# Attention values multiplied straight into token order, and the small items put at fewer places between the convolution's steps

## The reference

```
x = x + L0_conv(ln(x))      # spectral mixing
t = t + L0_ffn(ln(t))       # 8 experts, top 2
x = x + L1_conv(ln(x))      # the block that this change is in
t = t + L1_ffn(ln(t))       # 8 experts, top 2, and one shared expert
```

```
y    = relu(conv3x3(x, entry_w) * entry_s + entry_b)      # 256 -> 128 channels
qv   = conv1x1(y, vqk_w, ...);  qh = conv1x1(y, hqk_w, ...)   # 16 channels each
A_v  = softmax over rows    of qv . qv, for each column
A_h  = softmax over columns of qh . qh, for each row
feat = conv1x1(y, val_w, val_s, val_b)                    # the values, 128 channels
s_v  = A_v @ feat;   x_v = s_v * gate_v(mean of s_v)
s_h  = A_h @ x_v;    x_h = s_h * gate_h(mean of s_h)
out  = concat(conv1x1(x_h, end_w, ...), conv1x1(mean(x), il_w, ...))
```

## Time and profile before

| | us |
|---|---|
| runs (three) | 1201.56, 1196.70, 1191.82 |
| median | 1196.7 |
| profiled execution | 1199.71 |
| its span, first to last instruction | 1197.3 |
| passes with convolution | 602 to 819 |
| pass 8 | 819 to 849 |
| passes 9 to 12 | 849 to 897 |

### The profile page before, as it was taken

How to read it: one execution, slowest core, us unless ns; L and a number is a source line. 1 busy time by engine, 2 the same in 40 slices (tenths; PEclk the granted TensorE clock), 3 DMA queues, 4 the chain that set the end, 5 groups by cost and what they waited for, 6 DMA issues and landing times. The chain is left out here.

```text
span 1197.3 us, 19835 instructions
## 1 busy us (share of the span) xinstructions
PE 1025.8 (86%) x5686; PEld 858.5 (72%) x5686; DVE 615.7 (51%) x1712; ACT 528.2 (44%) x1328; POOL 264.1 (22%) x274
## 2 busy tenths in 40 slices
PE   6956669999999999973489999998776799997897
PEld 6956658888888888862256665665535799986787
DVE  5488653323232322226356676555778355554566
ACT  6027264444444444432144344433335466666563
POOL 0000012111111111107522200000000554424655
PEclk9999999999999999995689999997665799998889
DMA  9533501111111111118222301002230344434444
GB/s 354 234 110 136 176 24 49 53 54 54 54 54 53 54 54 54 49 41 268 73 80 79 89 1 53 36 18 71 89 123 1 101 139 140 136 114 150 151 131 132
DMA packets 63237, 114.61 MB, mean 96 GB/s; under 512 B 9827, under 2 KB 43253, under 8 KB 62262
## 3 DMA queue, kind: packets, MB, share of 16 engines
q1 hardware_dynamic: 49910, 77.65, 18.5%
q0 software_dynamic: 12960, 35.41, 10.4%
q10 hardware_dynamic: 288, 0.47, 0.1%
HBM read 73.90 MB, written 39.59 MB: 95 GB/s over the span
## 5 line engine op out<-in xcount | busy, mean ns | idle before, releaser
L574 POOL DMA_INDIRECT experts_rows_sb<-h_rows,ids_i x142 | 134.6, 948 | 751.0 <-POOLq L402 423.1
L761 DVE TENSOR_TENSOR experts_a_sb<-experts_a_sb,experts_bankU 128x512 f32<-128x512 f32 x71 | 48.9, 689 | 224.1 <-PE experts_bankU L180 224.1
L714 ACT ACTIVATE experts_a_sb<-experts_bankG 128x512 f32<-128x512 f32 (+1 forms) x142 | 70.0, 493 | 93.0 <-PE experts_bankG L180 91.2
L705 ACT ACTIVATE experts_hT<-experts_bankH 128x256 fp32r<-128x256 f32 x142 | 54.5, 384 | 89.6 <-PE experts_bankH L634 89.5
L727 ACT ACTIVATE experts_y_sb<-experts_bankY 128x256 f32<-128x256 f32 x142 | 54.8, 386 | 87.7 <-PE experts_bankY L177 65.3
L178 PE MATMUL attn_bankC<-attn_padded,attn_w_high 128*128 128x512 f32 x144 | 76.4, 530 | 19.8 <-ACT attn_feat L1432 14.6
L1136 POOL DMA_INDIRECT attn_y<-y_rows,pos_i x64 | 63.9, 998 | 112.2 <-DVE x_res L1562 57.2
L834 POOL DMA_INDIRECT shared_y<-y_rows,pos_i x64 | 65.4, 1022 | 63.9 <-DVE x_res L943 32.1
L177 PE MATMUL experts_bankY<-down_plain,experts_aT_plain 128*128 x284 | 72.9, 379 | 0.0
L183 DVE TENSOR_TENSOR experts_aT<-experts_bankA,experts_aT 128x256 fp32r<-128x256 f32 x142 | 59.6, 420 | 24.1 <-ACT experts_aT L722 24.1
L641 PE MATMUL experts_bankA<-konst_sb,experts_a_sb 128*128 128x128 f32 x426 | 70.0, 273 | 0.4 <-DVE experts_aT L183 0.4
(11 more groups left out here) (365 smaller groups left out, 2853.5 us busy)
## 6 DMA issues: line engine op xcount, KB each, us to landing
y_rows<-experts_y_sb SPq DMA_DIRECT2D x142, 128.0 KB, 1.7
h_rows<-xn SPq DMA_DIRECT2D x32, 256.0 KB, 2.4
x_res<-in_x SPq DMA_DIRECT2D x4, 1024.0 KB, 12.3
mix_xT<-in_xt SPq DMA_DIRECT2D x4, 1024.0 KB, 14.1
gate_raw<-in_L_ffn_gate_w SPq DMA_DIRECT2D x1, 4096.0 KB, 14.2
up_raw<-in_L_ffn_up_w SPq DMA_DIRECT2D x1, 4096.0 KB, 23.5
x_rows<-x_res SPq DMA_DIRECT2D x16, 256.0 KB
x_res<-x_rows SPq DMA_DIRECT2D x8, 512.0 KB, 4.6
```

What stands on the lines that cost most here:

```text
L574: nc.gpsimd.indirect_dma_start(rows[t % DEPTH][:, :], None, h_dram, bass.IndirectOffsetOnAxis(ap=ids_i[:, t:t + 1], axis=0)).then_inc(s_ro ...
L714: nc.scalar.activation(a_sb[i % RING][:, :], bankG[i % RING][:, 0:hidden], ACT.Silu if gate is not None else ACT.Relu).then_inc(s["act"], 1)
L761: nc.vector.tensor_tensor(a_sb[i % RING][:, :], a_sb[i % RING][:, :], bankU[i % RING][:, 0:hidden], ALU.mult).then_inc(s["a"], 1)
```

## The change

The values are made with tokens on the partitions at once. `feat` is written in column order (the ReLU copy is two activations of 256 columns). `project_values` loads blocks of `feat` and streams `val_w`: a bias matmul first, then four products, in the form of `finish`. The value scale is multiplied into `val_w` in `tables`, the bias goes into a third section of `bias_rows`. The transposes of the values, their buffer `val_t` and their semaphore are gone; `values` is the ReLU itself. As `feat` is in column order, the `down` queries are copied by one activation of 512, the `along` queries by two of 256 that go back to row order: three activations where there were five. Two small loads (`val_sb`, `out_rows`) are dropped, `scales_b` is half as wide again.

The small items stand at 8 places between steps of the convolution instead of 15, after every second step.

```diff
                 def project_values(p):
...
-                    nc.tensor.matmul(bankF[:, :], val_w[:, :], feat[:, :], start=True, stop=True).then_inc(s["projected"], 1)
+                    nc.tensor.matmul(bankF[:, :], ones2[:, :], bias_rows[:, 2 * F:3 * F].unsqueeze(1).broadcast_to([2, 4, F]), start=True, stop=False)
+                    for t in range(4):
+                        last = nc.tensor.matmul(bankF[:, t * P:(t + 1) * P], feat[:, t * P:(t + 1) * P], val_w[:, :], start=False, stop=(t == 3))
+                    last.then_inc(s["projected"], 1)
...
-                def turn_values(p):
-                    if not has(p):
-                        return
-                    for t in range(4):
-                        last = nc.tensor.transpose(bankV[:, t * P:(t + 1) * P], val_t[:, t * P:(t + 1) * P], K("ident"))
-                    last.then_inc(s["values_t"], 1)
...
                     finish(i - 4)
                     convolve(i, 0, 2)
                     gate_layer(i - 2, 0)
-                    convolve(i, 2, 3)
                     project_queries(i - 1)
-                    convolve(i, 3, 4)
                     project_values(i - 1)
-                    convolve(i, 4, 5)
+                    convolve(i, 2, 4)
                     turn_rows(i - 5, 0)
                     gate_layer(i - 2, 1)
-                    convolve(i, 5, 7)
+                    convolve(i, 4, 6)
                     turn_rows(i - 5, 1)
                     gate_layer(i - 2, 2)
-                    convolve(i, 7, 8)
                     scores(i - 1, "down")
-                    convolve(i, 8, 9)
+                    convolve(i, 6, 8)
                     turn(i + 1, 0)
                     route(i - 5, 0, 0)
                     gate_layer(i - 2, 3)
-                    convolve(i, 9, 10)
                     scores(i - 1, "along")
-                    convolve(i, 10, 11)
+                    convolve(i, 8, 10)
                     route(i - 5, 0, 1)
+                    route(i - 5, 1, 0)
                     gate_layer(i - 2, 4)
-                    route(i - 5, 1, 0)
-                    convolve(i, 11, 12)
-                    turn_values(i - 1)
+                    convolve(i, 10, 12)
                     route(i - 5, 1, 1)
-                    convolve(i, 12, 13)
                     branch(i)
                     gate_layer(i - 2, 5)
-                    convolve(i, 13, 14)
+                    convolve(i, 12, 14)
                     turn(i + 1, 1)
                     turn_probs(i - 1, "down")
                     turn_logits(i - 5)
-                    convolve(i, 14, 15)
                     turn_probs(i - 1, "along")
-                    convolve(i, 15, 16)
+                    convolve(i, 14, 16)
                     turn_gated(i - 2)
-                    convolve(i, 16, 17)
                     attend_down(i - 1)
-                    convolve(i, 17, 18)
+                    convolve(i, 16, 18)
                     attend_along(i - 2)
...
-                    nc.scalar.activation(feat[:, :], bankC[:, :], ACT.Relu, bias=entry_sb[:, 1:2], scale=entry_sb[:, 0:1]).then_inc(s["feat"], 1)
+                    for n in range(2):
+                        part = slice(n * 256, (n + 1) * 256)
+                        last = nc.scalar.activation(feat[:, part].rearrange("p (h y z) -> p h y z", h=2, y=ROWS), by_column(bankC[:, part]), ACT.Relu,
+                                                    bias=entry_sb[:, 1:2], scale=entry_sb[:, 0:1])
+                    last.then_inc(s["feat"], 1)
...
+                    nc.scalar.activation(q["down"][:, :], bankQ[0:G, :], ACT.Relu, bias=qk_sb[0:G, 1:2], scale=qk_sb[0:G, 0:1])
                     for n in range(2):
                         part = slice(n * 256, (n + 1) * 256)
...
-                    nc.scalar.activation(q["along"][:, :], bankQ[32:32 + G, :], ACT.Relu, bias=qk_sb[32:32 + G, 1:2],
-                                         scale=qk_sb[32:32 + G, 0:1]).then_inc(s["queries"], 1)
+                        last = nc.scalar.activation(by_column(q["along"][:, part]), bankQ[32:32 + G, part].rearrange("p (h y z) -> p h y z", h=2, y=ROWS),
+                                                    ACT.Relu, bias=qk_sb[32:32 + G, 1:2], scale=qk_sb[32:32 + G, 0:1])
+                    last.then_inc(s["queries"], 1)
...
-                    nc.scalar.activation(val[:, :], bankV[:, :], ACT.Copy).then_inc(s["values"], 1)
+                    nc.scalar.activation(val[:, :], bankF[:, :], ACT.Relu).then_inc(s["values"], 1)
...
                     nc.vector.tensor_tensor(end_w[:, :], end_w[:, :], scales_b[:, 0:F], ALU.mult)
+                    nc.vector.tensor_tensor(val_w[:, :], val_w[:, :], scales_b[:, 2 * F:3 * F], ALU.mult)
```

More of the change, by code:

```diff
@@ L977, in attention @@
             s = {n: sem(f"attn_{n}") for n in ("border", "w_high", "w_low", "mask", "tables", "sum", "chain", "var", "log", "root", "rstd", "xn", "turned", "high", "lows", "conv",
-                                               "feat", "projected", "queries", "values_t", "values", "probs_sb", "along_sb", "att",
+                                               "feat", "projected", "queries", "values", "probs_sb", "along_sb", "att",
                                                "att_sb", "row_sums", "gated", "gated_t", "gated_sb", "att2", "feat2", "col_sums",
@@ L1033, in attention @@
             table = {"down": "same_col", "along": "same_row"}
-            bias_raw = sb("attn_bias_raw", [2, 2 * F], on=on)
-            bias_part = [sb(f"attn_bias_part{n}", [2, 2 * F], HALF, on=on) for n in range(2)]
-            bias_rows = sb("attn_bias_rows", [2, 2 * F], HALF, on=on)
+            bias_raw = sb("attn_bias_raw", [2, 3 * F], on=on)
+            bias_part = [sb(f"attn_bias_part{n}", [2, 3 * F], HALF, on=on) for n in range(2)]
+            bias_rows = sb("attn_bias_rows", [2, 3 * F], HALF, on=on)
             ones2 = sb("attn_ones2", [2, P], HALF, on=on)
@@ L1042, in attention @@
             bankP = {"down": bankQ, "along": bankF}
-            bankV, bankO, bankE = bankF, bankS["down"], bankS["along"]
+            bankO, bankE = bankS["down"], bankS["along"]
             GATES = PAIRS + 1
@@ L1096, in _ @@
                 load_x(1)
-                sp.dma_start(bias_raw[:, :], A["out_rows"][:, 2 * F:4 * F].broadcast_to([2, 2 * F])).then_inc(loads["attn"], 16)
+                sp.dma_start(bias_raw[:, :], A["out_rows"][:, 3 * F:6 * F].broadcast_to([2, 3 * F])).then_inc(loads["attn"], 16)
                 load_attention(sp)
@@ L1453, in queries @@
                     act.wait_ge(s["projected"], p + 1)
-                    if p:
-                        act.wait_ge(s["values_t"], p)
+                    nc.scalar.activation(q["down"][:, :], bankQ[0:G, :], ACT.Relu, bias=qk_sb[0:G, 1:2], scale=qk_sb[0:G, 0:1])
                     for n in range(2):
                         part = slice(n * 256, (n + 1) * 256)
-                        nc.scalar.activation(q["down"][:, part].rearrange("p (h y z) -> p h y z", h=2, y=ROWS),
-                                             by_column(bankQ[0:G, part]), ACT.Relu, bias=qk_sb[0:G, 1:2], scale=qk_sb[0:G, 0:1])
-                        nc.scalar.activation(val_t[:, part].rearrange("p (h y z) -> p h y z", h=2, y=ROWS),
-                                             by_column(bankF[:, part]), ACT.Relu, bias=val_sb[:, 1:2], scale=val_sb[:, 0:1])
-                    nc.scalar.activation(q["along"][:, :], bankQ[32:32 + G, :], ACT.Relu, bias=qk_sb[32:32 + G, 1:2],
-                                         scale=qk_sb[32:32 + G, 0:1]).then_inc(s["queries"], 1)
+                        last = nc.scalar.activation(by_column(q["along"][:, part]), bankQ[32:32 + G, part].rearrange("p (h y z) -> p h y z", h=2, y=ROWS),
+                                                    ACT.Relu, bias=qk_sb[32:32 + G, 1:2], scale=qk_sb[32:32 + G, 0:1])
+                    last.then_inc(s["queries"], 1)
                 def values(p):
@@ L2273, in layouts @@
         "il_w": t(a["L1_conv_il_w"].reshape(KC, P, F).transpose(1, 0, 2).reshape(P, -1)),
-        "out_rows": t(np.concatenate([a[f"L1_conv_{n}"] for n in ("end_s", "il_s", "end_b", "il_b")])[None]),
+        "out_rows": t(np.concatenate([a[f"L1_conv_{n}"] for n in ("end_s", "il_s", "val_s", "end_b", "il_b", "val_b")])[None]),
         "L1_ffn_w_router": by_contracted_row(a["L1_ffn_w_router"][None]),
```

17 lines of the change are left out of this document (6 added, 11 removed).

## The result

| | before | after |
|---|---|---|
| median of 20 runs, us | 1194.14 (1187.80 to 1201.56) | 1184.43 (1176.71 to 1193.11) |
| ratio, 95% interval | 1 | 0.991 (0.9888 to 0.9932) |
| span of the profiled execution, us | 1197.3 | 1181.4 |

The two spans differ by 15.9 us, so a part of that difference is not in the medians. I split the spans in three. Up to the first convolution of pass 1: 601.93 before, 597.45 after (-4.5). From there to the first routing matmul: 301.26 and 292.97 (-8.3). The rest: 294.11 and 290.98 (-3.1). The middle part holds the edited passes. Of the edit only small things lie ahead of it: the feature copy of pair 0, the scaling of `val_w` and two loads fewer.

A forecast was written before the change was run, and what follows sets the result against it. TensorE was taken to bound the passes with convolution, chains of three engines pass 8. Terms -4.0 + 1.4 - 1.0 - 1.65 + 0.7 + 0.2 = -4.35 us off the median 1196.7 gave 1192.4, range 1185 to 1201.

The forecast's parts named there:

- breaks: Fewer breaks between convolution steps save TensorE 0.67 us in passes 2 to 4, 0.96 in 5 to 7, 0.10 in 1.
- stall: TensorE waits 0.35 us for VectorE's `leaky` of layer 4, ahead of gate layer 5, in passes 2 and 4: +0.7 us.
- not kept: Gains at the end of passes 4 and 5 are lost waiting for VectorE's sums at gate layer 0: +0.2 us.
- row waits: Waits for copied rows, about 0.32 us each in passes 5 to 7, go with ScalarE's shorter query chain: -1.0 us.
- feature copy: Splitting ScalarE's copy in two delays the next pass's convolution by 0.24 us in each of six passes: +1.4 us.
- The signs: Passes 5 and 6 0.6 to 1.0 us shorter; wrong if seven passes move over 6 us or change lies outside 602-897.
- Rival 1: Grouped items on TensorE still pay their breaks: it loses 1.0 us instead of gaining 4.0, 1197.4 us; chance 0.22.
- The direct values on TensorE: Bias matmul and four products cost 1.43 us against 1.29 for old matmul and transposes: 0.14 more per pair.
- Pass 8: Shorter ScalarE chain less later values gives -0.6 us, transposes gone at half clock give -1.05: together -1.65 us.
- Rival 3: TensorE keeps full clock in pass 8 after a wait of 2.2 us, giving back 5 to 6 us: 1186.5; chance 0.14.
- Rival 2: ScalarE's feature copy and VectorE's gate chain bound each pass: +2.2 to +3.8 us, 1199 to 1200.5; chance 0.14.
- Rival 4: ScalarE's idle times in the last stage that no engine releases move, 5 us either way: 1187 or 1198; chance 0.12.

The follow-up runs named there:

- places alone: The kernel before with the 8 places of the new order, values still transposed: 1153.14 us, ratio to before 0.9892, and 0.9888 when timed again.
- values alone: The kernel after with the 15 places of before, so only the direct values are new: 1166.16 us, ratio to before 1.0011.
- e4: The kernel before with only `attend_down` moved ahead of step 17 of the convolution, 14 places: 1190.96 us, before 1191.04 on that chip.
- e8: Places alone with `attend_down` moved behind the convolution's last step in passes 1 to 3: 1152.73 us, ratio to before 0.9885.
- e5: The kernel before with the ReLU feature copy in two activations of 256 columns, row order kept: 1195.46 us, before 1191.04 on that chip.

## Why the prediction was right or wrong

What failed, in short. The sum has two halves. The terms of the places (breaks -5.0, stall +0.7, not kept +0.2) make -4.1 us; on the second kind of chip places alone measured -13.0 and -13.3 (the medians above). The terms of the direct values (+1.0, +1.4, -1.0, -1.65) make -0.25; alone they measured -0.3 (1.0011, interval 0.9993 to 1.0030), but on top of the places +6.6. So the places were priced too low, and the values added on top too favourably; on those chips the two misses partly cancel (-6.5 for the whole, -4.35 forecast), which is luck.

Three steps inside the passes are named below: the move of `attend_down` was put at nothing without a reason (0.75 us), a wait was priced by the idle time shown (0.32 for 0.49), and costs were charged where they arise though a later wait takes them in (0.5). In the profiles of places alone 8.4 and 7.4 us of the gain lie in passes 1 to 7 and 3.6 and 5.5 in passes 8 to 12 (against the second execution of before); there the granted clock differs (in pass 8 0.71 and 0.84, against 0.61), and how much of that is the change's is open. The 7.4 are accounted for nearly in full: the 4.1 forecast, 1.5 of row waits (which the sum had with the values, at 1.0), 0.75 by `attend_down` and the stall of 0.7 that places alone hasn't got make 7.05. And 2.6 us of the distance from the forecast 1192.4 aren't the change's: it was taken off a median of three runs, 1196.7, and that of twenty is 1194.1.

By its own sum, pass by pass (the forecast of each is its terms added up; the feature copy's sixth 0.24 lies ahead of pass 1):

| pass | forecast | after - before, first executions | second executions |
|---|---|---|---|
| 1 | +0.28 | -0.39 | -0.09 |
| 2 | +0.06 | -0.19 | -0.41 |
| 3 | -0.29 | -0.37 | -0.34 |
| 4 | +0.06 | -0.02 | -0.01 |
| 5 | -0.81 | -1.57 | -1.56 |
| 6 | -1.05 | -1.69 | -1.73 |
| 7 | -1.15 | -2.29 | -2.28 |
| 8 | -1.65 | -2.81 | -3.89 |

**The signs.** The prediction named passes 1 to 7 moving by more than 6 us together as a sign of being wrong: they moved by 6.5. So did a change outside the edited stretch: 7.6 us of the first two spans lie there. Passes 5 and 6 got shorter by 1.6 and 1.7 us, not by 0.6 to 1.0, and pass 1 got shorter, not longer. The transposes are gone from pass 8, and its wait on the rows is 1.93 (2.2 forecast).

**The breaks: right in the price of each.** Priced as in the prediction, pass 7's items between convolution steps came to 15.57 us before and to 14.10 with places alone. Of the 1.47 gained, 0.51 is the row wait (second rows and layer 2 took 1.37, first rows and layer 1, which don't wait, 0.86; below). The rest, 0.96, is what was forecast, in part by luck, as the terms show. Junction by junction: gate layer 0, queries and values 2.27 where they were 0.54 + 1.19 + 0.86 (-0.32, forecast 0.29); layer 2 and scores 2.19 for 0.86 + 1.50 (-0.17; 0.19); layer 3 and scores 2.28 for 0.94 + 1.50 (-0.16; 0.19); transposes, route, branch and layer 5 2.40 for 1.16 + 1.43 (-0.19; 0.19); route next to route 1.38 for 1.48 (-0.10, which I had not counted); the turned probabilities -0.05 (0.10); two full-array items next to each other +0.03 (0). Rival 1, that the breaks don't pay, fell. By the rule on changes of tiling mode (the Trainium skill, "TensorEngine Tiling (Array Packing)", section "Key Properties") a group of unlike items would have kept its drains, and the sum by it was 0.27 us for a late pass. The trace doesn't agree with that sum: 0.96.

**The direct values on TensorE: right alone, too dear in the group.** With their own break they cost 1.49 against 0.86 + 0.44 for matmul and transposes, +0.19 (forecast +0.14, bound 0.23). In the group of after, 2.74 - 2.27 = 0.47 is paid for 0.45 saved (2.40 - 1.95 where the transposes stood): +0.02.

**The row waits: right that they end, the price too low, the second cause missed.** I put their end down to ScalarE's shorter chain. Values alone bears that out, but places alone ends them too, which I had not seen: the two edits share one gain. And I took the idle time shown, 0.32 us, for the price. TensorE of before, pass 5:

```profile
730.12 0.43 PE L180 MATMUL attn_bankC<-attn_padded,attn_w_low 128*128 128x512 f32 x1
730.87 0.63 PE L1297 MATMUL attn_bankT<-konst_sb,xn 128*128 128x128 f32 x4 [0.32 <-ACT moe_xT L1441]
```

From start to start it is 0.75, where a full-array item enters at 0.26: the wait costs 0.49. The profile counts idle time from the modelled end of the matmul before; in a stream the next would have started before that end. Three waits give 1.5 and not 1.0 us.

**The feature copy: right in size, wrong in where it is paid.** By itself it puts +0.23 ahead of five passes, as forecast; in passes 5 and 6 it is taken out of a wait that follows, 0.24 each, so about 0.5 us too much was charged. The wait that is late next was in the earlier trace rows, and I used it only against the gains. In after the wait ahead of pass 2 even fell, from 3.29 to 2.73, as it did with places alone (2.72): ScalarE starts that copy 26.35 us after pass 1's first matmul where it was 26.97. No term had this.

**What was left out: `attend_down`, -0.75 in pass 7.** The diff moves it one step forward, and the sum has no term for the move: TensorE does the same work. VectorE's chain behind it ends the pass. In the profile it was to be seen as idle time of VectorE behind L1226, followed by 4.54 us without a gap.

**Pass 8: the terms right, the clock left out of the sum.** Up to the second rows: 5.84 us before, 5.39 after, -0.45 (forecast -0.6). From the route behind these scores to gate layer 5, where the transposes of the values stood: 7.97 and 6.84, -1.13 (-1.05). From there to pass 9: +0.18. What is left of the -2.81 lies between. TensorE of after:

```profile
814.98 0.63 PE L1292 MATMUL attn_bankT<-konst_sb,xn 128*128 128x128 f32 x4 [1.93 <-ACT moe_xT L1432]
...
816.11 1.33 PE L1203 MATMUL attn_bankS_down<-attn_q_down 16*128 16x128 f32 x8
817.37 1.02 PE L1304 MATMUL attn_bankX<-moe_xT,router_sb 128*8 128x256 f32 x2
818.33 0.42 PE L1242 MATMUL attn_bankG<-attn_hidden,gates_wh 64*64 64x32 f32 x2
818.68 0.79 PE L1199 MATMUL attn_bankS_along<-attn_mask_along_r,attn_mask_along_l 9*128 9x512 f32 x1
819.27 1.90 PE L1203 MATMUL attn_bankS_along<-attn_q_along 16*128 16x128 f32 x8
```

The four transposes take 0.63 us where they took 1.09 in before: the clock is still at 2.4 GHz. The mask matmul further on takes 0.79 (0.50 at full clock): 1.2 GHz. From the second rows to the route behind the scores it is 2.39 us, 3.80 before: -1.41. The full clock lasted 2 us longer, not to the end of the pass. Rival 3 put this down to the shorter wait. The record doesn't bear that out. TensorE of e4, with the old values and a wait as long as in before:

```profile
820.61 0.63 PE L1297 MATMUL attn_bankT<-konst_sb,xn 128*128 128x128 f32 x4 [2.83 <-ACT moe_xT L1440]
821.16 0.30 PE L1247 MATMUL attn_bankG<-attn_hidden,gates_wh 64*64 64x32 f32 x2
821.39 0.50 PE L1197 MATMUL attn_bankS_down<-attn_mask_down_r,attn_mask_down_l 9*128 9x512 f32 x1
```

The full clock outlasts the wait of 2.83 us here, and so it does in e8, in both executions of places alone and in e5, which has the order and the waits of before (0.63 us for the transposes in each). Pass 8 has a mean granted clock of 0.66 and 0.61 in the two executions of before, 0.70 in e4 and 0.76 in e5, which have its wait, 0.71, 0.84 and 0.76 (e8) with places alone, 0.68 in three of after, and 0.80 with values alone (25.65 us). So these 1.4 us belong to the executions that were profiled; that the change brings them isn't shown.

**The wait for `leaky` of layer 4: right in size, half right in place.** 0.29 us in pass 4 (forecast 0.35); none in pass 2, and none at all with places alone. Rival 2 fell: the stall is well under its 0.6 us.

**Outside the edited stretch.** In the first executions 7.6 us of the 15.9 lie ahead of pass 1 and behind pass 12; in the second ones after is 1.5 us shorter ahead and 0.5 longer behind. ScalarE's idle times marked remote come to 20.1 us in one piece before pass 1 in before and to 16.5 in two in after; in four more executions on such a chip they range from 3.8 to 23.8 (the last section). So I take the 7.6 us for differences between executions. Rival 4, that the change moves these idle times, isn't excluded, and the smaller gain on the chips that have none (0.9947 for 0.991) would fit it too; that stays open.

**The sum of the misses.** Passes 1 to 8 were forecast at -4.55 and gave -9.3 in the first executions. Of the 4.8 between, 1.15 is pass 8 (1.4 by the clock, less 0.25 by which its other parts fell short), 0.75 `attend_down`, 0.8 the values (seven times 0.12 too dear), 0.5 the feature copy, 0.5 the row waits and 0.4 the wait for `leaky`: 4.1. The rest is within what passes 1 to 3 vary, and pass 1 has the shorter wait ahead of pass 2. The errors nearly all had one sign.

**What else is open.** After is 6.6 us slower than places alone in the medians. The profiles hold 0.6 to 0.9 us of it in passes 2 to 7 (184.42 and 184.65, against 183.80 in the execution in which pass 3 is at the same clock), and about 1 us behind pass 12; passes 8 to 12 go the other way (80.8 and 78.7, against 80.9 and 79.0). Pass 3 took 28.75 us at full clock in two of three profiled executions with the old values and the new places, and 30.5 in all six with the direct values and the new order; pass 1 took 29.2 and 29.6 at a clock of 0.90 and 0.85 in two of seven with the direct values, and 26.8 to 27.9 elsewhere. Such a lean of the clock would fill much of the gap. So few executions can't show whether it does.

**The better version.** The 8 places with the values transposed as before: 1153.14 us against 1166.17 to 1166.47, ratio 0.989, and 6.6 us under the kernel after on the same chips.

## What to carry to other kernels

Small matmul items between the steps of a long stream cost 0.1 to 0.2 us here each time the stream was left and entered (0.96 us for seven breaks less in pass 7); gather them, and place the gap after the producer so that the other engine's chain fits in. A wait ahead of a matmul in such a stream is dearer than the idle time shown (0.49 for 0.32 us): read it from start to start. When an item moves, ask which engine's gapless chain it releases, and read that engine's idle time at it; when a copy gets slower, find the wait that follows and may absorb it. Test two edits that come together one at a time: here one carried all of the gain and the other gave a part of it back.

## What the hardware showed that I had not expected

**The clock moves whole passes.** Pass 3 with places alone, behind a wait of 2.04 and 2.05 us, in two executions (columns as in the earlier trace rows; the clock is the last but two). The first:

```profile
641.50:670.25 28.75, 28.36 (x146) 20.10 (x147) 19.08 (x59) 12.46 (x38) 7.65 (x8) 1.00 0.32 92
```

The other:

```profile
641.34:671.68 30.34, 29.98 (x146) 20.61 (x147) 19.18 (x59) 12.47 (x38) 7.69 (x8) 0.94 0.29 88
```

The same work takes 1.6 us more at a mean granted clock of 0.94. A clock that falls in only some executions of one kernel is no property of the order; only repeated executions tell the two apart.

**Chips differ in how long ScalarE stands still ahead of the stage.** The kernel before has a median of 1194 us on one kind of chip and 1166 on another. ScalarE's waits before pass 1, on the first:

```profile
ACT attn_padded L1423 <- remote: 20.1, 1, 20.1
ACT attn_log L1405 <- DVE attn_var L1581: 10.9, 2, 7.3
```

and in the execution on the second:

```profile
ACT attn_log L1405 <- DVE attn_var L1581: 11.8, 2, 7.1
ACT attn_xn L1397 <- DVE attn_bias L1594: 5.1, 3, 2.3
```

The profile names no engine or DMA that releases it in the first ("remote"); in the second there is none. Pass 1 begins at 601.9 and at 584.5, and the part behind the edited stretch is 294 and 280 us: together all of the difference of 30 us between the two spans. The other executions divide the same way: all six on chips of the first kind have such idle times, 3.8 to 23.8 us ahead of pass 1 and 15 to 22 in the last stage, and none of the eight on the second kind has any. They aren't the whole of it: in e4, with 3.8 us ahead of pass 1, that pass still begins at 595.7. What the idle time is, no run here shows.
